# A new order of the ticks on every engine, in a transformer between two ternary FFNs

## The chip, the cores and the metric

One core of a Trainium2 chip. The time is that of the device in microseconds; before the change the median of three runs is 927.53 us (926.24 to 928.54).

## The reference, cut to what matters

The input is 16 sequences of 256 tokens, 128 features, in fp32: 4096 tokens, which the kernel cuts into 8 tiles of 512 tokens (two sequences each). Three parts follow one another, each with a residual:

```
x = x + 0.5 * ffn(layernorm(x))             # "input FFN"
x = x + layers(layernorm(x))                # 8 layers
x = x + 0.5 * ffn(layernorm(x))             # "output FFN"

def ffn(x):     # w_q is ternary: -1, 0, 1 by a threshold of mean |w|
    h = gelu(x / (rms(x) + eps) @ w_up_q.T)          # 128 -> 512, erf form
    return h / (rms(h) + eps) @ w_down_q.T           # 512 -> 128

for each of the 8 layers:
    Q = elu(x @ Wq + bq) + 1;  K = elu(x @ Wk + bk) + 1;  value = x @ Wv + bv
    KV = sum over the sequence of K * value;  Ksum = sum of K
    V = Q * KV / (Q * Ksum + eps)
    x = layernorm(gelu(V @ Wo + bo) + x) * scale + bias      # tanh form
    x = layernorm(gelu(gelu(x @ W1 + b1) @ W2 + b2) + x) * scale + bias
```

The sums run over one sequence only, so tile t of a layer needs tile t of the layer before and nothing else.

## The kernel before, in words

Layer work is 64 jobs (8 layers of 8 tiles), taken two at a time in 32 ticks. Each engine has a function that emits one tick (`tensor_tick`, `scalar_tick`, `vector_tick`, `gpsimd_tick`), and its last part is a list of calls, written out by hand. The queue of an engine is this list, tick after tick; it is worked off in order, and semaphores are all that holds the engines together.

A call such as `z(l(0, 3), 1)` names a stage, a tile and for some stages a half of the layer (0 attention, 1 FFN) or a chunk. `tiles_of` turns `l(k, lag)` into job 2 * (tick - lag) + k of the layers, `a(k, lag)` into a tile of the input FFN, t = 2 * (tick - lag + 4) + k, and `b(k, lag)` into one of the output FFN, t = 2 * (tick - lag - 32) + k. Where the number is out of range the call emits nothing. So a lag says how many ticks after the first a stage comes. `rest` leaves out tile 0 of the input FFN, whose first stages stand ahead of the ticks.

The stages of a layer tile, in the order of data: TensorE projects K, Q and V (`project`, three passes each); ScalarE makes the negative part and its `exp`; VectorE makes `round_kq`, `phi_k`, `phi_q`, `sum_kv` and the small `neg_ksum`, `over_ksum`, `sum_value`, `mean_v`; ScalarE `log_den` and `recip` (the reciprocal by ln and exp); VectorE `attend`; TensorE `project_o`; ScalarE `gelu_o`; VectorE `residual` 0; TensorE transposes (`turn_y`); VectorE `stats` and `means`; GpSimd `var_eps` and `rstd`; VectorE `z` (normalises, reading PSUM); TensorE turns back (`turn_z`); `full` applies scale and bias (ScalarE for half 0, VectorE for half 1); VectorE `hi` rounds and GpSimd `low` (L1303) takes the rest, for products in two parts; TensorE `up` (four chunks), ScalarE `gelu_h`, TensorE `down`, ScalarE `gelu_ff`, and from `residual` 1 on as above. GpSimd also splits the weights of the next layer, one piece (a cast, L1260, and a subtraction, L1262) behind `low(l(0, 3), 1)` and one behind it for the other tile.

An outer FFN tile: (`enter`, `x_in` at the output FFN: turns the layers' result and adds it to the token rows) `outer_stats`, `outer_means`, `var_eps`, GpSimd `sd` and `sd_eps`, VectorE `alpha`, ScalarE `normal`, TensorE `turn`, ScalarE `z_hi` (L678), VectorE `z_lo` (L953), TensorE `outer_up` (L531, L532), ScalarE `gelu` and `square`, VectorE `add_squares` (which sums the four chunks of squares into one, L1093 and L1095), TensorE `squares`, VectorE `mean_square`, GpSimd `rms`, VectorE `beta`, TensorE `outer_down` in two halves (L544), VectorE `outer_residual` (L1120). The input FFN goes on with `stats_c`, `means_c`, `rstd_c`, `z_c`, `turn_c`, `enter_full`, `enter_hi` and GpSimd's `x_low` (L1349), which together are the layer norm ahead of the layers.

The 8 banks of PSUM are shared: the dictionary `left` holds, for each bank, which semaphore says that it was drained, and `emptied` waits for it. SyncE only loads weights and inputs and stores the output; the change does not touch it. Where ScalarE goes over between `exp`/`ln` and a gelu, or between the two gelus, a table is loaded.

The lags before: input FFN -30 to -20, layers -1 to 3, output FFN 17 to 22, ticks from -34 to 57. Layer calls are in ticks -1 to 34, calls of the output FFN in ticks 49 to 57.

Of the kernel before, what the change touches and what calls it, by code (L numbers as in the profile page):

```python
# [680 lines left out]
def scalar_tick(act, m, s, f, tick, tables):  # L681
# [120 lines left out]
    gelu(b(1, 22), 0)
    gelu_h(l(1, 2), 1)
    z_hi(act, m, rest(a(1, -29)))
    gelu_ff(l(0, 2))
    gelu_o(l(1, 1))
    gelu_h(l(1, 2), 2)
    gelu(b(1, 22), 1)
    gelu_h(l(1, 2), 3)
    gelu(a(0, -29), 2)  # L810
    z_hi(act, m, b(0, 21))
    gelu(b(1, 22), 2)
    gelu(a(0, -29), 3)
    full(l(0, 1), 0)
    gelu(b(1, 22), 3)
# [13 lines left out]
    gelu(b(0, 21), 0)
    gelu(a(1, -29), 1)  # L830
    gelu(b(0, 21), 1)
    enter_full(a(0, -21))
    normal(act, m, rest(a(1, -30)))
    z_hi(act, m, b(1, 21))
    gelu_ff(l(1, 2))
    gelu(b(0, 21), 2)
    gelu(b(0, 21), 3)
    enter_hi(a(0, -21))
# [118 lines left out]
def vector_tick(dve, m, s, f, tick):  # L957
# [194 lines left out]
    add_squares(a(1, -27))  # L1152
    stats(l(1, 2), 0)
    means(l(0, 3), 1)
    round_kq(l(0, 0))
    over_ksum(l(1, 1))
    mean_square(b(0, 21))
    z_lo(dve, m, b(0, 20))
    x_in(b(1, 18))
    means(l(1, 2), 0)  # L1160
    phi_q(l(0, 0))
    outer_stats(dve, m, rest(a(0, -30)))
    beta(b(0, 21))
    alpha(dve, m, rest(a(0, -29)))
    beta(a(0, -27))
    outer_residual(a(0, -27))
# [242 lines left out]
```

## Time and profile before

| | us |
|---|---|
| median of three runs | 927.53 |
| lowest, highest | 926.24, 928.54 |
| the profiled execution | 928.71 |
| its span, first to last instruction | 926.9 |
| VectorE busy in the span | 823.6 (89%) |
| TensorE busy, matmuls | 855.2 (92%) |
| ScalarE busy | 795.8 (86%) |
| GpSimd busy | 443.4 (48%) |
| mean granted TensorE clock | 0.959 |

The busy shares are means over very unlike stretches: the opening and the input FFN (to about 108 us), the filling of the layers, the steady ticks, their drain (to about 839 us) and the output FFN. A granted clock of 1.00 is 2.4 GHz, 0.50 is 1.2 GHz. Names in rows are those of the buffers: `mv` is written by `means`, `st` by `stats`, `y` by `residual`, `kv` by `sum_value`, `nks` by `neg_ksum`, `fz_c` by `z_c`, `x_lo` by `low` or `x_low`, `x_tm` by `x_in` (L1085) or `outer_residual` (L1120).

### The profile page before, as it was taken

The numbers are of one execution on the slowest core, as the hardware profiler recorded it, in microseconds if no ns is written. First come the engines' busy times: TensorE is split into PE (matmuls) and PEld (weight loads), VectorE is DVE, ScalarE is ACT, GpSimd is POOL, SyncE is SP. The second block draws the span as 40 slices with busy tenths as digits, with TensorE's granted clock in tenths as the row PEclk, the third lists the DMA queues.
The fourth block names the chain that finished last, engine by engine and source line by source line (L and its number), as shares of the span: only waits on it lengthen the run. The fifth ranks groups of instructions, "written<-read, shape, count | busy, mean of one in ns | idle before, by whom it ended". The sixth has DMA issues, their size and how long they took to land.

```text
span 926.9 us, 14284 instructions
## 1 busy us (share of the span) xinstructions
PE 855.2 (92%) x3915; PEld 601.6 (65%) x3915; DVE 823.6 (89%) x3349; ACT 795.8 (86%) x1138; POOL 443.4 (48%) x561
## 2 busy tenths in 40 slices
PE   3898469999999999999999999999999999985897
PEld 2788245666666666666666666666666666654786
DVE  6677567999999999999999999999999999966663
ACT  3784579999999999999999999999999999733871
POOL 3253512555555555555555555555555555333230
PEclk8799789999999999999999999999999999995998
DMA  5000000000000000000000000000000000000011
GB/s 153 1 8 3 27 0 10 1 15 1 21 1 16 13 10 0 15 13 10 3 14 21 1 15 0 21 1 16 12 0 1 1 1 1 1 0 1 24 35 35
DMA packets 19518, 12.04 MB, mean 13 GB/s; under 512 B 1160, under 2 KB 18288, under 8 KB 19440
## 3 DMA queue, kind: packets, MB, share of 16 engines
q1 hardware_dynamic: 19440, 11.13, 4.2%
q8 instruction: 33, 0.54, 0.2%
q14 instruction: 45, 0.37, 0.1%
HBM read 9.03 MB, written 2.10 MB: 12 GB/s over the span
## 4 chain that ended last, share of the span: by engine, by line
DVE 69%; PE 12%; ACT 9%; issue 8%; POOL 2%; DMA 0%; DVEq 0%; ACTq 0%; POOLq 0%
DVE z L859 16%; DVE st L845 10%; DVE x_fm L1069 5%; DVE phi_k L982 5%; DVE kvf L993 4%; DVE phi_q L972 4%; DVE mv L852 4%; DVE e L965 4%; DVE vf L1034 3%; DVE x_hi L1077 3%; PE bank L544 3%; PE bank L394 2%; DVE y L1042 2%; ACT hsq L771 2%; ACT fh L764 2%
## 5 line engine op out<-in xcount | busy, mean ns | idle before, releaser
L1303 POOL TENSOR_TENSOR x_lo<-x_fm,x_hi 128x512 fp32r<-128x512 f32 x120 | 155.5, 1306 | 259.3 <-DVE x_hi L1077 259.3
L495 PE MATMUL bank<-h,w 128*128 128x512 f32 x512 | 260.5, 593 | 0.0
L737 ACT ACTIVATE h<-bank,par 128x512 f32<-128x512 f32 x256 | 167.1, 693 | 11.6 <-PE bank L402 10.6
L859 DVE TENSOR_SCALAR z<-bank,mv,rstd 128x128 f32<-128x128 f32 x512 | 169.2, 401 | 8.4 <-POOL rstd L1295 8.2
L400 PE MATMUL bank<-x_hi,w_hi 128*128 128x512 f32 x256 | 151.6, 592 | 1.6 <-ACT h L737 1.6
L1295 POOL TENSOR_TENSOR rstd<-ve,minus_half 128x4 f32<-128x4 f32 x128 | 132.8, 1037 | 10.7
L400 PE MATMUL bank<-x_hi,wqkv_hi 128*128 128x512 f32 x192 | 107.5, 560 | 11.2 <-DVE phi_q L972 10.1
L845 DVE BATCH_NORM_STATS2 st<-bank 128x6 f32<-128x128 f32 x512 | 112.8, 281 | 1.0 <-PE bank L394 0.9
L394 PEld LDWEIGHTS bank<-ident,y 128*128 128x128 f32 x512 | 62.3, 141 | 59.9 <-ACT x_fm L753 23.4
L402 PE MATMUL bank<-x_hi,w_lo 128*128 128x512 f32 x256 | 101.2, 395 | 0.0
L401 PE MATMUL bank<-x_lo,w_hi 128*128 128x512 f32 x256 | 101.1, 395 | 0.0
L495 PEld LDWEIGHTS bank<-h,w 128*128 128x128 f32 x512 | 86.9, 190 | 14.3 <-issue 3.4
L692 ACT ACTIVATE e<-bank,par 128x512 f32<-128x512 f32 x128 | 85.6, 693 | 8.0 <-PE bank L402 7.8
L1042 DVE TENSOR_TENSOR y<-bank,x_fm 128x512 f32<-128x512 f32 x128 | 86.9, 682 | 5.0 <-ACT bank L729 4.6
L1289 POOL TENSOR_SCALAR ve<-mv 128x4 f32<-128x4 f32 x128 | 49.5, 387 | 83.3 <-DVE mv L852 77.8
L656 ACT ACT_TABLE_LOAD x63 | 80.8, 1283 | 1.1
L394 PE MATMUL bank<-ident,y 128*128 128x128 f32 x512 | 77.4, 274 | 3.3 <-DVE y L1042 2.2
L737 ACT ACT_TABLE_LOAD x61 | 78.3, 1283 | 1.1
L402 PE MATMUL bank<-x_hi,wqkv_lo 128*128 128x512 f32 x192 | 78.0, 406 | 0.0
L401 PE MATMUL bank<-x_lo,wqkv_hi 128*128 128x512 f32 x192 | 78.0, 406 | 0.0
L400 PEld LDWEIGHTS bank<-x_hi,w_hi 128*128 128x128 f32 x256 | 48.6, 190 | 42.4 <-issue 17.2
L394 PE MATMUL bank<-ident,z 128*128 128x128 f32 x512 | 67.8, 275 | 7.4 <-DVE z L859 7.4
(102 smaller groups left out, 1780.7 us busy)
## 6 DMA issues: line engine op xcount, KB each, us to landing
x_tm<-in_x SPq DMA_DIRECT2D x8, 256.0 KB, 4.0
raw_w<-in_W SPq DMA_DIRECT2D x8, 256.0 KB, 2.7
w<-in_W SPq DMA_DIRECT2D x8, 256.0 KB, 2.9
out<-x_tm SPq DMA_DIRECT2D x8, 256.0 KB, 2.3
raw_qkv<-in_Wk SPq DMA_DIRECT2D x8, 64.0 KB, 2.0
raw_qkv<-in_Wq SPq DMA_DIRECT2D x8, 64.0 KB, 2.4
raw_qkv<-in_Wv SPq DMA_DIRECT2D x8, 64.0 KB, 2.3
wo<-in_Wo SPq DMA_DIRECT2D x8, 64.0 KB, 2.5
```

The source lines that it names most:

```text
L394: last = pe.transpose(bank[:, j * P:(j + 1) * P], src(j), m.ident[:, :])
L400: pe.matmul(bank[:, :], w_hi, x_hi, start=True, stop=False)
L401: pe.matmul(bank[:, :], w_hi, x_lo, start=False, stop=False)
L402: return pe.matmul(bank[:, :], w_lo, x_hi, start=False, stop=True)
L495: mm = pe.matmul(m.ps_o[:, :], m.w2[T.weights][:, c, :], m.h[:, T.par, c, :], start=c == 0, stop=c == FC - 1)
L692: act.activation(m.e[:, T.par, i, :], bank[:, :], ACT.Relu, bias=column(m, base, T.layer), scale=-1.0).then_inc(done, 1)
L737: act.activation(m.h[:, T.par, c, :], m.ps_h[c % 2][:, :], ACT.Gelu_apprx_tanh, bias=column(m, B1, T.layer, c, FC)).then_inc(s.gelu_h[T.pa ...
L845: last = dve.bn_stats(st[:, j, :], src(j))
L859: last = dve.tensor_scalar(dst[:, j, :], src(j), mv[:, j, 0:1], scale[:, j:j + 1], ALU.subtract, ALU.mult)
L1042: dve.tensor_tensor(m.y[i][:, T.par, :], (m.ps_v, m.ps_o)[i][:, :], m.x_fm[:, T.slot, :], ALU.add).then_inc((s.y1, s.y2)[i], 1)
L1295: pool.tensor_tensor(m.rstd[i][:, T.par, :], m.ve[i][:, T.par, :], m.minus_half[:, :], ALU.pow).then_inc((s.rstd1, s.rstd2)[i], 1)
L1303: pool.tensor_tensor(m.x_lo[:, T.slot, :], m.x_fm[:, T.slot, :], m.x_hi[:, T.slot, :].bitcast(F32), ALU.subtract).then_inc(done, 1)
```

## The change

It replaces the four lists, and the constants that say where the ticks begin and end. The stage functions, the buffers, the work of SyncE and what lies ahead of the ticks stay as they are, and each list has the same calls as before for the layers and both FFNs, in another order and with other lags. The lags now: input FFN -24 to -15, layers -2 to 3 (-2 only for one ScalarE call), output FFN -1 to 4; ticks from -28 to 39. So the calls of the output FFN stand in ticks 31 to 39, and the layers' in -2 to 34: in ticks 31 to 34 the lists of all engines hold both. The first layer's weight splits on GpSimd move from tick -29 to -23.

The constants, the new list of VectorE whole, before it that of TensorE whole, between them some lines of ScalarE's, and at the end that of GpSimd:

```diff
-TICK_QKV, TICK_W1 = -29, -29
-FIRST_TICK, END_TICK = -34, 58
+TICK_QKV, TICK_W1 = -23, -23
+FIRST_TICK, END_TICK = -28, 40
...
+    turn(pe, m, b(1, 3), left)
+    turn_z(l(0, 1), 0)
+    up(l(1, 2), 3)
+    turn_z(l(1, 3), 1)
+    outer_up(b(0, 3), 1)
+    outer_up(a(0, -21), 0)
+    outer_down(a(0, -20), 1)
+    outer_up(a(0, -21), 1)
+    project(l(1, 0), VALUE)
+    turn(pe, m, rest(a(1, -21)), left)
+    turn_c(a(1, -17))
+    squares(b(1, 4))
+    outer_up(b(0, 3), 2)
+    turn_y(l(0, 2), 1)
+    project(l(0, -1), KEY)
+    outer_up(b(0, 3), 3)
+    turn_y(l(1, 1), 0)
+    outer_up(a(0, -21), 2)
+    enter(b(0, -1))
+    project(l(0, -1), QUERY)
+    outer_down(b(1, 4), 0)
+    down(l(1, 2), 0)
+    outer_up(a(0, -21), 3)
+    outer_up(b(1, 3), 0)
+    squares(a(1, -20))
+    up(l(0, 1), 0)
+    outer_down(a(1, -20), 0)
+    outer_down(b(1, 4), 1)
+    outer_up(a(1, -21), 0)
+    outer_down(a(1, -20), 1)
+    down(l(1, 2), 1)
+    down(l(1, 2), 2)
+    outer_up(b(1, 3), 1)
+    turn(pe, m, b(0, 2), left)
+    project(l(0, -1), VALUE)
+    down(l(1, 2), 3)
+    outer_up(a(1, -21), 1)
+    outer_up(b(1, 3), 2)
+    outer_up(b(1, 3), 3)
+    project(l(1, -1), KEY)
+    enter(b(1, -1))
+    squares(b(0, 3))
+    project(l(1, -1), QUERY)
+    up(l(0, 1), 1)
+    up(l(0, 1), 2)
+    turn_z(l(1, 1), 0)
+    turn_z(l(0, 2), 1)
+    project_o(l(0, 0))
+    up(l(0, 1), 3)
+    outer_down(b(0, 3), 0)
+    turn(pe, m, rest(a(0, -22)), left)
+    turn_y(l(1, 2), 1)
+    down(l(0, 1), 0)
+    outer_up(a(1, -21), 2)
+    outer_up(b(0, 2), 0)
+    outer_up(a(1, -21), 3)
+    turn_y(l(0, 0), 0)
+    turn_c(a(0, -18))
+    outer_down(b(0, 3), 1)
+    down(l(0, 1), 1)
+    project_o(l(1, 0))
+    up(l(1, 1), 0)
+    down(l(0, 1), 2)
+    up(l(1, 1), 1)
+    down(l(0, 1), 3)
+    up(l(1, 1), 2)
+    squares(a(0, -21))
+    outer_down(a(0, -21), 0)
...
+    gelu(b(0, 3), 3)
+    square(b(0, 3))
+    exp(l(1, -1))
...
+    normal(act, m, b(0, 2))
+    gelu(b(1, 3), 0)
...
+    z_hi(act, m, b(0, 2))
...
+    square(a(0, -21))
+    gelu(b(1, 3), 2)
+    normal(act, m, rest(a(0, -22)))
+    gelu(b(1, 3), 3)
+    gelu(a(1, -21), 0)
...
+    normal(act, m, rest(a(1, -22)))
+    normal(act, m, b(1, 2))
...
+    z(l(0, 3), 1)
+    outer_stats(dve, m, rest(a(1, -23)))
+    mean_v(l(1, 1))
+    var_eps(dve, m, b(1, 2))
+    sum_kv(l(0, 0))
+    mean_square(a(1, -20))
+    attend(l(1, 1))
+    residual(l(1, 3), 1)
+    alpha(dve, m, b(0, 2))
+    z_lo(dve, m, rest(a(1, -21)))
+    means_c(a(1, -19))
+    stats_c(a(0, -20))
+    alpha(dve, m, rest(a(0, -22)))
+    hi(l(1, 2), 0)
+    full(l(0, 3), 1)
+    residual(l(0, 1), 0)
+    stats(l(1, 3), 1)
+    beta(a(1, -20))
+    hi(l(0, 3), 1)
+    means(l(1, 3), 1)
+    sum_value(l(0, 0))
+    over_ksum(l(0, 0))
+    stats(l(0, 1), 0)
+    add_squares(a(0, -21))
+    means(l(0, 1), 0)
+    z_lo(dve, m, b(1, 3))
+    var_eps_c(a(0, -19))
+    outer_stats(dve, m, b(1, 1))
+    z(l(1, 3), 1)
+    mean_v(l(0, 0))
+    x_in(b(1, 0))
+    beta(b(1, 4))
+    z(l(0, 1), 0)
+    round_kq(l(1, 0))
+    residual(l(1, 1), 0)
+    add_squares(b(0, 3))
+    alpha(dve, m, rest(a(1, -22)))
+    var_eps_c(a(1, -19))
+    phi_k(l(1, 0))
+    outer_residual(b(1, 4))
+    outer_means(dve, m, rest(a(0, -23)))
+    outer_means(dve, m, b(0, 1))
+    residual(l(0, 2), 1)
+    outer_residual(a(1, -20))
+    neg_ksum(l(1, 0))
+    var_eps(dve, m, rest(a(0, -23)))
+    full(l(1, 3), 1)
+    hi(l(0, 1), 0)
+    alpha(dve, m, b(1, 2))
+    outer_means(dve, m, rest(a(1, -23)))
+    z_lo(dve, m, rest(a(0, -22)))
+    z_c(a(0, -19))
+    mean_square(a(0, -21))
+    var_eps(dve, m, rest(a(1, -23)))
+    phi_q(l(1, 0))
+    sum_kv(l(1, 0))
+    mean_square(b(0, 3))
+    over_ksum(l(1, 0))
+    hi(l(1, 3), 1)
+    z_lo(dve, m, b(0, 2))
+    add_squares(b(1, 3))
+    stats(l(0, 2), 1)
+    outer_stats(dve, m, rest(a(0, -24)))
+    stats_c(a(1, -20))
+    stats(l(1, 1), 0)
+    beta(a(0, -21))
+    sum_value(l(1, 0))
+    add_squares(a(1, -21))
+    attend(l(0, 0))
+    means(l(1, 1), 0)
+    beta(b(0, 3))
+    round_kq(l(0, -1))
+    means(l(0, 2), 1)
+    x_in(b(0, -1))
+    outer_residual(b(0, 3))
+    var_eps(dve, m, b(0, 1))
+    phi_k(l(0, -1))
+    outer_stats(dve, m, b(0, 0))
+    outer_means(dve, m, b(1, 1))
+    outer_residual(a(0, -21))
+    z_c(a(1, -19))
+    means_c(a(0, -20))
+    phi_q(l(0, -1))
+    mean_square(b(1, 3))
+    z(l(1, 1), 0)
+    neg_ksum(l(0, -1))
...
+    sd(b(1, 2))
+    var_eps(l(0, 1), 0)
+    sd_eps(b(1, 2))
+    sd_eps(a(1, -23))
+    rstd(l(0, 1), 0)
+    low(l(0, 3), 1)
+    rms(a(1, -21))
+    split_next_qkv(l(0, 0))
+    split_next_w1(l(0, 0))
+    rms(b(0, 3))
+    split_next_qkv(l(1, 0))
+    split_next_w1(l(1, 0))
+    low(l(0, 1), 0)
+    rstd_c(a(0, -20))
+    sd(b(0, 1))
+    low(l(1, 3), 1)
+    rstd_c(a(1, -20))
+    var_eps(l(1, 1), 0)
+    rstd(l(1, 1), 0)
+    sd(a(0, -24))
+    var_eps(l(0, 2), 1)
+    rstd(l(0, 2), 1)
+    sd_eps(b(0, 1))
+    x_low(a(1, -15))
+    rms(a(0, -22))
+    low(l(1, 1), 0)
+    var_eps(l(1, 2), 1)
+    sd_eps(a(0, -24))
+    sd(a(1, -24))
+    rms(b(1, 3))
+    rstd(l(1, 2), 1)
+    x_low(a(0, -16))
```

## Rows read from the trace of the kernel before

**Rows 1.** The page, 40 slices of the span, busy tenths of VectorE.
```profile
DVE  6677567999999999999999999999999999966663
```
**Rows 2.** Stretches: bounds and length in us, then busy us (x instructions) of PE, PEld, DVE, ACT, POOL.
```profile
0.00:160.00 160.00, 113.86 (x590) 89.88 (x591) 107.41 (x429) 106.00 (x158) 58.77 (x80) 0.86 0.10 29
160.00:782.00 622.00, 622.00 (x2676) 419.90 (x2674) 620.31 (x2562) 608.44 (x856) 340.14 (x430) 1.00 0.03 8
782.00:839.00 57.00, 49.84 (x208) 31.66 (x207) 45.54 (x177) 31.53 (x45) 20.72 (x27) 0.95 0.00 1
839.00:853.00 14.00, 7.22 (x29) 5.25 (x29) 10.46 (x50) 4.42 (x10) 5.92 (x6) 0.50 0.00 1
853.00:927.00 74.00, 62.30 (x418) 54.86 (x416) 39.89 (x135) 45.40 (x72) 17.84 (x18) 0.92 0.09 29
```
**Rows 3.** Instructions in time order, VectorE: start us, us, line and operation [idle before].
```profile
261.98 0.72 DVE L972 SCALAR_TENSOR_TENSOR phi_q<-bank,par,e 128x512 f32<-128x512 f32 x1
```
**Rows 4.** The same view, one steady tick of VectorE.
```profile
459.26 2.63 DVE L859 TENSOR_SCALAR z<-bank,mv,rstd 128x128 f32<-128x128 f32 x8
461.82 0.47 DVE L982 SCALAR_TENSOR_TENSOR phi_k<-bank,par,e 128x256 f32<-128x256 f32 x1
...
474.17 0.21 DVE L1015 SCALAR_TENSOR_TENSOR kv<-ksum,par,kvacc 128x2 f32<-128x2 f32 x1
...
474.36 0.68 DVE L1042 TENSOR_TENSOR y<-bank,x_fm 128x512 f32<-128x512 f32 x1
...
479.27 0.88 DVE L845 BATCH_NORM_STATS2 st<-bank 128x6 f32<-128x128 f32 x4
480.18 0.38 DVE L852 BATCH_NORM_AGGREGATE mv<-st 128x2 f32<-128x6 f32 x4
480.48 0.72 DVE L972 SCALAR_TENSOR_TENSOR phi_q<-bank,par,e 128x512 f32<-128x512 f32 x1
```
**Rows 5.** The same view, VectorE in the drain, the last layer tile.
```profile
833.64 0.38 DVE L852 BATCH_NORM_AGGREGATE mv<-st 128x2 f32<-128x6 f32 x4
835.49 1.36 DVE L859 TENSOR_SCALAR z<-bank,mv,rstd 128x128 f32<-128x128 f32 x4 [1.47 <-POOL rstd L1295]
```
**Rows 6.** The same view, VectorE and GpSimd at the end of the input FFN.
```profile
95.21 1.12 DVE L859 TENSOR_SCALAR fz_c<-x_tm,fmv_c,frstd_c 128x128 f32<-128x128 f32 x4
96.53 4.88 DVE L859 TENSOR_SCALAR fz_c<-x_tm,fmv_c,frstd_c 128x128 f32<-128x128 f32 x4 [0.20 <-POOL frstd_c L1341]
...
96.39 9.87 POOL L1349 TENSOR_TENSOR x_lo<-x_fm,x_hi 128x512 fp32r<-128x512 f32 x8
```
**Rows 7.** The same view, GpSimd in a steady tick: the cast of a weight split.
```profile
461.35 0.29 POOL L1260 CAST w_hi<-raw_w 128x128 fp32r<-128x128 f32 x1
```
**Rows 8.** The same view, TensorE and VectorE between layers and output FFN.
```profile
837.00 1.08 PE L394 MATMUL bank<-ident,z 128*128 128x128 f32 x4 [4.45 <-DVE z L859]
837.88 1.06 PE L394 MATMUL bank<-ident,x_fm 128*128 128x128 f32 x4
...
852.95 0.78 PE L531 MATMUL bank<-zc_hi,upT 128*128 128x512 f32 x1
...
838.13 0.81 DVE L1069 TENSOR_SCALAR x_fm<-bank,par 128x512 f32<-128x512 f32 x1 [1.27 <-PE bank L394]
```
**Rows 9.** The same view, the output FFN at its pace, and the last residual.
```profile
883.72 0.50 PE L531 MATMUL bank<-zc_hi,upT 128*128 128x512 f32 x1 [0.99 <-DVE zc_lo L953]
...
898.83 0.51 PE L531 MATMUL bank<-zc_hi,upT 128*128 128x512 f32 x1 [0.98 <-DVE zc_lo L953]
...
922.79 1.12 DVE L1120 SCALAR_TENSOR_TENSOR x_tm<-bank,scale,x_tm 128x128 f32<-128x128 f32 x4 [5.26 <-PE bank L544]
```
**Rows 10.** Groups from 782 us on: line, engine, operation xcount | busy us, mean ns | idle before.
```profile
L678 ACT ACTIVATE zc_hi<-bank 128x512 fp32r<-128x512 f32 x8 | 4.8, 601 | 1.5 <-PE bank L394 1.5
...
L1085 DVE TENSOR_TENSOR x_tm<-bank,x_tm 128x512 f32<-128x512 f32 x8 | 5.5, 686 | 1.7 <-PE bank L394 1.6
L953 DVE TENSOR_TENSOR zc_lo<-bank,zc_hi 128x512 fp32r<-128x512 f32 x8 | 5.5, 686 | 2.8 <-ACT zc_hi L678 2.8
```

More of the change, by code:

```diff
@@ L802, in scalar_tick @@
[L802 to L815, printed above, removed]
     negative(l(0, -1), QUERY)
-    negative(l(0, -1), KEY)
+    recip(l(0, 0))
     exp(l(0, -1))
-    square(b(1, 22))
-    square(a(0, -29))
-    normal(act, m, b(1, 21))
@@ L822, in scalar_tick @@
-    normal(act, m, rest(a(0, -30)))
+    z_hi(act, m, rest(a(0, -21)))
+    gelu(b(0, 3), 0)
     log_den(l(1, 0))
-    recip(l(0, 0))
+    gelu(b(0, 3), 1)
     recip(l(1, 0))
-    gelu(a(1, -29), 0)
     gelu_h(l(0, 1), 0)
-    gelu_h(l(0, 1), 1)
[L829 to L838, printed above, removed]
@@ L839, in scalar_tick @@
-    negative(l(1, -1), QUERY)
-    enter_full(a(1, -21))
+    gelu_ff(l(1, 2))
+    z_hi(act, m, b(1, 3))
+    negative(l(1, -1), KEY)
+    gelu(a(1, -20), 2)
+    gelu(a(1, -20), 3)
+    gelu_h(l(0, 1), 1)
+    square(a(1, -20))
+    gelu_h(l(0, 1), 2)
+    gelu(b(0, 3), 2)
+    full(l(1, 1), 0)
+    gelu(a(0, -21), 0)
+    gelu(a(0, -21), 1)
+    gelu_o(l(0, 0))
+    enter_hi(a(1, -16))
+    negative(l(1, -1), QUERY)
+    gelu_h(l(0, 1), 3)
+    gelu(b(0, 3), 3)
+    square(b(0, 3))
+    exp(l(1, -1))
@@ new lines, in scalar_tick @@
+    z_hi(act, m, rest(a(1, -21)))
+    gelu_o(l(1, 0))
+    gelu_h(l(1, 1), 0)
+    gelu(a(0, -21), 2)
+    gelu_h(l(1, 1), 1)
+    normal(act, m, b(0, 2))
+    gelu(b(1, 3), 0)
+    gelu(a(0, -21), 3)
+    enter_full(a(0, -17))
+    gelu(b(1, 3), 1)
+    z_hi(act, m, b(0, 2))
+    enter_hi(a(0, -17))
+    gelu_ff(l(0, 1))
+    gelu_h(l(1, 1), 2)
+    full(l(0, 0), 0)
+    square(a(0, -21))
[3 more added lines that the diff above has]
+    gelu(a(1, -21), 0)
@@ L843, in block_stats @@
+    gelu_h(l(1, 1), 3)
+    gelu(a(1, -21), 1)
+    log_den(l(0, -1))
+    square(b(1, 3))
+    normal(act, m, rest(a(1, -22)))
+    normal(act, m, b(1, 2))
+    enter_full(a(1, -17))
+    negative(l(0, -2), KEY)
 def block_stats(dve, src, st, done):
@@ L1150, in z_c @@
         normalise(dve, m.fz_c[:, F.par], token_source(m, F), m.fmv_c[:, F.par], m.frstd_c[:, F.par], F.f.z_c)
[L1152 to L1166, printed above, removed]
@@ L1194, in vector_tick @@
     hi(l(1, 2), 0)
     full(l(0, 3), 1)
-    mean_square(b(1, 21))
+    residual(l(0, 1), 0)
     stats(l(1, 3), 1)
+    beta(a(1, -20))
     hi(l(0, 3), 1)
-    outer_means(dve, m, rest(a(0, -30)))
     means(l(1, 3), 1)
-    round_kq(l(1, 0))
-    x_in(b(0, 17))
-    var_eps(dve, m, rest(a(0, -30)))
-    stats(l(0, 1), 0)
-    means_c(a(0, -27))
-    means(l(0, 1), 0)
-    phi_q(l(1, 0))
-    outer_stats(dve, m, rest(a(1, -30)))
-    z(l(1, 3), 1)
-    z_lo(dve, m, b(1, 20))
-    z(l(0, 1), 0)
@@ L1212, in vector_tick @@
-    outer_stats(dve, m, b(1, 18))
-    phi_k(l(1, 0))
-    residual(l(0, 2), 1)
-    outer_residual(a(1, -27))
-    sum_value(l(0, 0))
-    residual(l(1, 1), 0)
-    neg_ksum(l(1, 0))
-    full(l(1, 3), 1)
-    mean_v(l(0, 0))
-    beta(b(1, 21))
-    hi(l(0, 1), 0)
-    mean_square(a(0, -28))
-    outer_means(dve, m, rest(a(1, -30)))
-    var_eps_c(a(0, -27))
-    stats_c(a(1, -27))
+    sum_value(l(0, 0))
[3 more added lines that the diff above has]
+    means(l(0, 1), 0)
@@ L1230, in vector_tick @@
-    z_lo(dve, m, rest(a(0, -29)))
-    outer_residual(b(1, 21))
-    add_squares(b(0, 20))
-    sum_kv(l(1, 0))
-    alpha(dve, m, b(1, 19))
-    var_eps(dve, m, b(0, 18))
-    var_eps(dve, m, rest(a(1, -30)))
-    add_squares(b(1, 20))
+    outer_stats(dve, m, rest(a(0, -24)))
[9 more added lines that the diff above has]
+    means(l(0, 2), 1)
```

123 lines of the change are left out of this document (removed).

## The prediction

> **What bounds the kernel now.** I read first the page's busy shares and 40 slices, then a table of stretches, then single instructions in time order. The slices of VectorE stand at 9 from about 140 us to 790 us and at 5 to 8 outside [rows 1]. The stretches say how full that is: from 160 to 782 us VectorE is busy 620.31 of 622 us and TensorE 622.00 of 622, ScalarE 608.44 [rows 2]. There the order can lose time and hardly win any. Outside, VectorE idles 160 - 107.4 = 53 us before 160 us, 57 - 45.5 = 11 us while the last layer drains, 3.5 us in the 14 us behind it and 74 - 39.9 = 34 us in the rest of the output FFN [rows 2]. All gains must come from these 101 us. One tick of two tiles is ten ticks apart at 261.98 and 480.48 us, so 21.85 us [rows 3, 4]; some 29 of them are in the steady stretch (622/21.85).
>
> **What the change keeps.** The steady lists have the same calls: 32 on TensorE, 24 on ScalarE, 40 on VectorE, and the same four activation-table loads a tick (two `exp` groups between gelus). Nothing is added or taken away, DMAs included; an empty entry of a tick issues nothing, so shorter lags (first tick -28, last 39) cost or save nothing by themselves. Everything is position within the queues.
>
> **Steady ticks, rstd waits: +6 us.** A normalisation `z` needs `rstd` of GpSimd, which needs `means`. A `means` started at 833.64 us and the `z` behind it at 835.49, with VectorE waiting 1.47 us for `rstd`: 1.85 us from start to start [rows 5]. In the old order `phi_q` or more stands between the two. In the new one, after `means(l(1,3),1)` come `sum_value`, `over_ksum`, `stats(l(0,1),0)`, `means(l(0,1),0)`, then `z(l(1,3),1)`. By start-to-start times of the trace: 0.30 (480.18 to 480.48) + 0.19 (474.17 to 474.36, `sum_value` and one such small instruction) + 0.91 (479.27 to 480.18) + 0.30 = 1.70 us [rows 4]. That is 0.15 us short of 1.85. Then `z(l(0,1),0)` stands 0.30 + 0.15 + 1.28 + 0.07 (the small `mean_v`, less than half of that 0.19) = 1.80 us behind the start of its own `means`, the 1.28 being half of 2.56 us for two `z` (459.26 to 461.82) [rows 4]: 0.05 us short. Together 0.20 us on a queue that has no slack: 29 x 0.20 = 6 us. Bounds: 0 (if a pair of instructions runs a little longer than my rows and covers it) and 0.3 a tick, 9 us. Other chains I compared in the same manner (`hi` after `full`, `turn_z` after `z`, the residual before the next `down`) have as much room as they had, and TensorE has the 0.20 us as slack then.
>
> **Steady ticks, GpSimd against VectorE: +1.5 us.** In the opening, `z_c` of one tile took 1.12 us, that of the next 4.88 us while GpSimd ran eight `x_low` back to back (9.87 us, 1.23 each): every quarter waited for one of them [rows 6]. So a VectorE instruction that reads and writes SBUF alone can be held up for the rest of a GpSimd instruction. Of this kind are `round_kq`, `hi` and `attend`. In the new tick, `low(l(0,3),1)` starts together with `z(l(0,1),0)`, both released by the same `rstd`; its follower on GpSimd, 1.23 us later, is the 0.29 us cast of a weight split [rows 6, 7], and `round_kq(l(1,0))` comes 1.28 us later [rows 4], 0.05 us into that cast. Cost between 0 and 0.3 us a tick. `hi(l(1,3),1)` follows `hi(l(0,1),0)` by `phi_q` and `sum_kv`, about as long as the `x_low` that the first one releases, so it may touch its end: 0 to 0.1 more. I take 0.05 a tick, since the two come so close that a shift of 0.3 us undoes it: 1.5 us; bounds 0 and 0.4 a tick, 12 us.
>
> The Trainium skill (SBUF — State Buffer, section "SBUF: two separate sides") says that the port pair shared by VectorE and GpSimd is an exclusive lock held for the whole instruction, the first to start winning and the other blocking. The trace agrees (4.88 against 1.12 us). It speaks against this change: taken to the letter, each tick would pay the rest of the cast at least, and that is the first rival below.
>
> **Drain, 782 to 839 us: +2.5 us.** `enter`, `x_in` and `outer_stats` of the output FFN now stand inside ticks 31 to 34, from lag -1 on. VectorE has 11 us of idle time there [rows 2]; TensorE 7. Before its last `down` TensorE gets five more `enter`: groups of four transposes start 0.88 us apart at half clock (837.00 to 837.88 [rows 8]), so 0.44 at full clock, 2.2 us, and a little where `x_in` stands before a `z`. Bounds 0 (hidden) and +6 (eight `x_in` of 0.69 us [rows 10] all on the chain, and some statistics).
>
> **The hand-over to the output FFN: -10 us.** Now the last `full` starts at 838.13 us, and the first `outer_up` at 852.95: 14.8 us in which six more `x_in`, statistics, roots, `alpha`, `normal`, `turn`, `z_hi` and `z_lo` of tile 0 pass one after another, TensorE at a granted 0.50, that is 1.2 GHz [rows 8, 2]. In the new lists tile 0 has had statistics and roots by tick 33, and `alpha`, `normal` run beside the last layer tile's chain of tick 34. What stays behind the last `turn_z` is, at half clock: `enter` of tile 6 (0.88), `turn` (1.08), `z_hi` 0.60, `z_lo` 0.69, `x_in` 0.69, `enter` of tile 7 (0.88) [rows 8, 10], 4.8 us, against 852.95 - 838.08 (end of the last `turn_z`) = 14.9. So -10. Bounds -6 and -13.
>
> **Pace of the outer FFNs: -4 us.** Two tiles take 898.83 - 883.72 = 15.1 us at the end, of which TensorE waits 0.98 us for `z_lo` [rows 9]. The new order puts `outer_down` of the other tile between `turn` and the `outer_up` that needs `z_lo`, which covers it: 14.1 to 14.4 us a pair, over three pairs of the output FFN and about as many of the input FFN, -2 us each. Bounds 0 and -8. The end is as before: `squares` and `outer_down` of the last tile behind `outer_residual` of the last but one, with the 5.26 us wait before the last residual [rows 9]. The first tile's gelu still stands behind `normal` of tile 1, and the eight `turn_c` still run after the last square: opening otherwise 0, with ±4 for it and for the filling of the layer pipeline, where even tiles now run half a tick earlier.
>
> **Sum.** 6 + 1.5 + 2.5 - 10 - 4 = -4 us. The profiled execution took 928.71 us (span 926.9, 1.8 around it), 1.2 above the median of 927.53: 924.7 for it, 923.5 for the median. I give 924.
>
> **Rivals.** (1) Slower: the exclusion of the two engines decides. If `round_kq(l(1,0))` waits 0.3 us in each tick and `hi` 0.1, with the 0.2 of `rstd` a tick is 22.45 us, +17 us; with +2.5 - 10 - 4 that is +6, 933 us. The change turns slower from 0.4 us a tick on (11.5/29). For it: the cast stands right at that place in every tick with a split; against: it is 0.29 us short, and the two starts need only drift 0.3 us apart. (2) The steady tick stays at 21.85, because small durations shift, and the rest comes: -11.5 to -16, 913 us. For it: GpSimd is half idle (340 of 622 us [rows 2]); against: 1.85 is measured on an idle GpSimd and can't be shorter. (3) The change doesn't overlap what it means to: the in-order queues couple drain and output FFN (`x_in` of tile 4 before `z(l(0,3),1)`), the drain grows by 6 to 8 us and eats the hand-over: 927 to 930.
>
> **Chances.** Forecast 0.45 (alone 919 to 929), rival 1 0.22, rival 2 0.20, rival 3 0.13. The range 910 to 934 leaves out the far ends of rivals 1 and 2. A measurement of this kernel tells 0.3%, 2.8 us, from no change: faster than 924.75 gets 0.26 of the forecast's 0.45, all of rival 2 and 0.03 of rival 3, 0.49; slower than 930.3 gets 0.02, 0.18 and 0.03, 0.23; the rest, 0.28, is within.
>
> **What would show it.** In the profile after: `phi_q` of one tile ten ticks apart by 220.5 us (22.05 a tick), with VectorE waits for `rstd` in the steady stretch, about two a tick and 0.15 and 0.05 us; `round_kq` rows that are longer than before are rival 1's. Some 4 to 6 us between the start of the last `full` and the first `outer_up` of the output FFN, where 14.8 stood. Pairs there 14.1 to 14.4 us apart. The forecast is wrong if the steady tick is under 21.9 or over 22.3 us, if the hand-over stays above 9 us, or if opening and filling move by more than 5 us.

## The result, and the profile after

The changed kernel takes 919.31 us (median of 7 runs, 918.08 to 923.22) against 927.14 for the kernel before (7 runs, 926.24 to 928.89): ratio 0.9918, 95% interval 0.9900 to 0.9936. The profiled execution took 919.31 us with a span of 917.5.

The slices of the page, to be read against [rows 1], and the stretches:

```profile
DVE  6688557999999999999999999999999999988674
PEclk9899569999999999999999999999999999999899
```

```profile
0.00:160.00 160.00, 117.12 (x601) 91.44 (x602) 110.05 (x443) 107.62 (x161) 60.19 (x81) 0.86 0.10 29
160.00:770.00 610.00, 609.75 (x2585) 405.83 (x2584) 606.56 (x2479) 592.15 (x826) 328.91 (x421) 1.00 0.03 8
```

VectorE is nearly as full as before (606.56 of 610 us, 99.4%; before 620.31 of 622, 99.7% [rows 2]), yet two tiles now take longer. One tile's `phi_q` starts at 199.97 and, 24 ticks later, at 732.19 us: 22.18 us a tick, where it was 21.85 [rows 3, 4]. The loss shows in VectorE's and GpSimd's rows of one tick, in order of time; idle time under a few tenths gets no bracket, so the reader subtracts starts:

```profile
479.91 0.37 DVE L852 BATCH_NORM_AGGREGATE mv<-st 128x2 f32<-128x6 f32 x4
480.19 0.18 DVE L1015 SCALAR_TENSOR_TENSOR kv<-ksum,par,kvacc 128x2 f32<-128x2 f32 x1
480.30 0.16 DVE L1008 RECIPROCAL nrk<-nks 128x2 f32<-128x2 f32 x1
480.38 0.87 DVE L845 BATCH_NORM_STATS2 st<-bank 128x6 f32<-128x128 f32 x4
481.28 0.38 DVE L852 BATCH_NORM_AGGREGATE mv<-st 128x2 f32<-128x6 f32 x4
481.75 1.37 DVE L859 TENSOR_SCALAR z<-bank,mv,rstd 128x128 f32<-128x128 f32 x4
483.03 0.15 DVE L1024 TENSOR_TENSOR neg_a<-kv,nrk 128x2 f32<-128x2 f32 x1
483.18 1.37 DVE L859 TENSOR_SCALAR z<-bank,mv,rstd 128x128 f32<-128x128 f32 x4
484.46 0.71 DVE L965 TENSOR_SCALAR e<-e 128x1024 f32<-128x1024 f32 x1
485.10 0.68 DVE L1042 TENSOR_TENSOR y<-bank,x_fm 128x512 f32<-128x512 f32 x1
```

```profile
480.67 1.04 POOL L1295 TENSOR_TENSOR rstd<-ve,minus_half 128x4 f32<-128x4 f32 x1
481.80 0.23 POOL L1289 TENSOR_SCALAR ve<-mv 128x4 f32<-128x4 f32 x1
482.11 1.04 POOL L1295 TENSOR_TENSOR rstd<-ve,minus_half 128x4 f32<-128x4 f32 x1
483.12 1.28 POOL L1303 TENSOR_TENSOR x_lo<-x_fm,x_hi 128x512 fp32r<-128x512 f32 x1
484.33 0.29 POOL L1260 CAST wqkv_hi<-raw_qkv 128x128 fp32r<-128x128 f32 x1
```

`means` at 481.28 is followed 0.47 us later, 0.30 in the order before [rows 4]: `z` waits 0.17 for the `rstd` that ends at 481.71. The small `mean_v` at 483.03 is followed after 0.15, not 0.07: the second `z` waits 0.08 for the `rstd` that ends at 483.15. The `round_kq` beside the cast is followed after 0.64 instead of 0.58. Averaged over 22 ticks of each profile, from start to start, it is +0.20 us a tick behind `means`, +0.08 behind `mean_v`, +0.06 behind `round_kq`, +0.05 behind the two `phi_q`, and -0.07 over all the rest: 0.32. These rows say where the time stands, not yet what taking one of them away would bring.

Behind the layers the time comes back. The last `full`, the first `outer_up` of the output FFN, and the last two residuals, against [rows 8, 9]:

```profile
847.22 0.81 DVE L1069 TENSOR_SCALAR x_fm<-bank,par 128x512 f32<-128x512 f32 x1 [0.39 <-PE bank L394]
```

```profile
851.98 0.78 PE L531 MATMUL bank<-zc_hi,upT 128*128 128x512 f32 x1
```

```profile
908.28 1.13 DVE L1120 SCALAR_TENSOR_TENSOR x_tm<-bank,scale,x_tm 128x128 f32<-128x128 f32 x4
...
913.41 1.13 DVE L1120 SCALAR_TENSOR_TENSOR x_tm<-bank,scale,x_tm 128x128 f32<-128x128 f32 x4 [2.43 <-PE bank L544]
```

The balance of the two profiles, in us, from such starts (before, after): up to the first `round_kq` 108.39, 104.05, that is -4.3; from there to the `phi_q` of job 11, counted from 0, some five ticks on (the "tenth" of two expectations below), 109.9, 118.1, +8.2 (6.6 of it beside five times 0.32); from that to the last job's `phi_q` (26 ticks) 568.0, 576.3, +8.3; drain to the last `full` 51.9, 48.8, -3.1; to the first `outer_up` 14.8, 4.8, -10.1; from it to the first residual 17.8, 15.4, -2.4; six more residuals 44.1, 40.9, -3.2; to the last one 8.0, 5.1, -2.8. Sum -9.4, as the spans.

The granted clock goes with the loss of the filling. The 24 us from the first `round_kq` on, first in the kernel before, then in the changed one (the last number but two is the clock):

```profile
108.00:132.00 24.00, 12.18 (x32) 7.09 (x32) 14.15 (x55) 16.53 (x23) 0.38 (x2) 0.86 0.09 25
104.00:128.00 24.00, 15.40 (x32) 9.37 (x32) 13.19 (x55) 13.96 (x20) 0.00 (x0) 0.51 0.08 24
```

### The profile page after: what moved, and what is told of

Read it like the earlier page. It is cut to its first block, busy times and chain, and to the rows that moved or that the text cites. A ratio compares the mean times of both kernels' runs of the same rounds, so it can differ in the third digit from the quotient of the medians.

```text
span 917.5 us, 14284 instructions
## 1 busy us (share of the span) xinstructions
PE 857.4 (93%) x3915; PEld 596.7 (65%) x3915; DVE 830.0 (90%) x3349; ACT 800.4 (87%) x1138; POOL 441.2 (48%) x561
## 4 chain that ended last, share of the span: by engine, by line
DVE 67%; PE 16%; issue 6%; ACT 5%; POOL 5%; DMA 0%; SPq 0%; DVEq 0%; ACTq 0%; POOLq 0%
DVE z L859 15%; DVE st L845 8%; DVE y L1042 8%; PE bank L544 6%; DVE phi_k L982 5%; DVE phi_q L972 4%; DVE e L965 4%; DVE x_fm L1069 4%; POOL rstd L1295 4%; DVE kvf L993 4%; DVE x_hi L1077 3%; DVE vf L1034 3%; DVE mv L852 3%; PE bank L394 2%; PE bank L531 2%
## 5 line engine op out<-in xcount | busy, mean ns | idle before, releaser
L1303 POOL TENSOR_TENSOR x_lo<-x_fm,x_hi 128x512 fp32r<-128x512 f32 x120 | 153.6, 1280 | 225.5 <-DVE x_hi L1077 225.5
L495 PE MATMUL bank<-h,w 128*128 128x512 f32 x512 | 255.5, 592 | 0.0
L859 DVE TENSOR_SCALAR z<-bank,mv,rstd 128x128 f32<-128x128 f32 x512 | 174.0, 403 | 7.9 <-POOL rstd L1295 5.2
L737 ACT ACTIVATE h<-bank,par 128x512 f32<-128x512 f32 x256 | 169.5, 690 | 9.1 <-PE bank L402 7.9
L400 PE MATMUL bank<-x_hi,w_hi 128*128 128x512 f32 x256 | 160.9, 629 | 0.0
L1295 POOL TENSOR_TENSOR rstd<-ve,minus_half 128x4 f32<-128x4 f32 x128 | 132.7, 1037 | 10.7
L400 PE MATMUL bank<-x_hi,wqkv_hi 128*128 128x512 f32 x192 | 108.6, 565 | 12.7 <-DVE phi_k L982 11.9
L495 PEld LDWEIGHTS bank<-h,w 128*128 128x128 f32 x512 | 91.7, 189 | 31.3 <-issue 17.5
L845 DVE BATCH_NORM_STATS2 st<-bank 128x6 f32<-128x128 f32 x512 | 109.8, 281 | 2.2 <-PE bank L394 2.2
L1289 POOL TENSOR_SCALAR ve<-mv 128x4 f32<-128x4 f32 x128 | 39.9, 312 | 129.2 <-DVE mv L852 124.1
L394 PE MATMUL bank<-ident,z 128*128 128x128 f32 x512 | 73.9, 277 | 9.0 <-DVE z L859 9.0
L394 PEld LDWEIGHTS bank<-ident,z 128*128 128x128 f32 x512 | 59.5, 141 | 29.4 <-DVE z L859 11.2
```

Source lines behind the costliest of these rows:

```text
L394: last = pe.transpose(bank[:, j * P:(j + 1) * P], src(j), m.ident[:, :])
L400: pe.matmul(bank[:, :], w_hi, x_hi, start=True, stop=False)
L495: mm = pe.matmul(m.ps_o[:, :], m.w2[T.weights][:, c, :], m.h[:, T.par, c, :], start=c == 0, stop=c == FC - 1)
L737: act.activation(m.h[:, T.par, c, :], m.ps_h[c % 2][:, :], ACT.Gelu_apprx_tanh, bias=column(m, B1, T.layer, c, FC)).then_inc(s.gelu_h[T.pa ...
L845: last = dve.bn_stats(st[:, j, :], src(j))
L859: last = dve.tensor_scalar(dst[:, j, :], src(j), mv[:, j, 0:1], scale[:, j:j + 1], ALU.subtract, ALU.mult)
```

## The experiments

**The three parts by themselves.** The lists of each engine were spliced: input FFN, layers and output FFN from either kernel.

```diff
 # e3: input and output FFN of the kernel before; layers' calls in the new order
 # e6: the kernel before; only the input FFN's calls a(...) in the new order,
 #     with their new lags and first tick
 # e4: the changed kernel, output FFN behind the layers
-    outer_up(b(0, 3), 1)
+    outer_up(b(0, 21), 1)      # all b(...) of all engines by +18 ticks
```

> The kernel before with only the calls of the layers in the new order; the input FFN ahead of them and the output FFN behind them keep their old order, and nothing of the output FFN stands inside the layers. Theory: this part alone is a loss: 31 ticks of +0.32 us = +10, a filling that takes +5, a drain of -3: 927 + 12 = 937 to 941 us; tick 22.17. Rival 1 (the loss of the filling is only the price of the earlier start of the layers, that is of something late that both kernels wait for): the filling costs 0 to 1 here and the time is 933 to 936. Rival 2 (the longer tick comes of the empty or changed surroundings, or of another placement in the run): tick 21.85 and 926 to 928.

Measured: 940.41 us, ratio 1.0143 (1.0123 to 1.0163), so +13 us, as expected. Tick 22.17, first `round_kq` at 108.28 as before, job 11's `phi_q` 8.2 us later than before, drain 48.0. The loss of the filling is not a price of an earlier start: rival 1 falls. The new order of the layers is a loss wherever it stands.

> The kernel before with the calls of the input FFN alone in their new order; the layers and the output FFN keep the old one. Theory (three parts that add up): the opening gains 4 to 6 us up to the first round_kq (108.4 us before, 101.7 to 104.1 in the four profiles with the new order), and because the layers' filling and steady stretch are those of before, all of it reaches the end: 922 to 924 us. Rival (the filling takes it back: what comes later is bound by something else than the input FFN): 926 to 928 us, with the first phi_q early and the tenth where it was, at 218.3 us.

Measured: 924.16 us (919.94 to 925.21), ratio 0.9961 (0.9946 to 0.9976): -2.4 us between the medians, -3.6 by the ratio. The profiled run is one of the quickest, 920.12. In its profile the first `round_kq` is at 102.13, and the last `full` at 832.83, 5.3 us earlier than before: in this run what the input FFN gained reached the last `full`. Over all runs it is 2 to 4 us.

> The changed kernel with the lags of all calls of the output FFN raised by 18 ticks, so that it stands wholly behind the layers, in its new order. Theory (the overlap gives the hand-over, the order gives the pace and the end): from the last full to the first outer_residual 30 to 33 us instead of 20.1, that is +10 to +12; the drain 0 to 2 us shorter; then pairs of 13.7 us and a last residual 5.1 us behind the one before as in the changed kernel: 929 to 931 us. Rival (pace and end are gained because the overlap keeps TensorE's granted clock up): pairs of 15 us and 8 us at the end as well, 935 to 938 us.

Measured: 932.00 us, 1.0056 (1.0039 to 1.0073), 12.7 above the changed kernel. From the last `full` at 844.29 to the last residual at 926.05 it takes 81.8 us, not 66.2. All 15.6 us lie ahead of the first residual: the seven gaps behind it are those of the changed kernel (7.3 and 6.4, the last 5.1). So the overlap makes the hand-over, and the order makes the pace. From the last `full` to the first residual it takes 35.7 us, where 30 to 33 stood: the granted clock is 0.50 all the way from 840 to 860 us here, and eight `enter` pass one by one, seven of them waiting for an `x_in`. How much of the 15.6 is the low clock and how much the overlap is not told apart here; a pair of runs with the clock up, below, does that.

**Where the tick loses.** One call of VectorE's list is moved into the wait for `rstd`.

```diff
     means(l(0, 1), 0)
+    round_kq(l(1, 0))
     ...
     z(l(0, 1), 0)
-    round_kq(l(1, 0))
```

> The changed kernel with one VectorE call moved: round_kq(l(1, 0)) goes from behind z(l(0, 1), 0) to ahead of z(l(1, 3), 1), right behind means(l(0, 1), 0). Theory (waits for rstd): the two normalisations come 1.84 and 1.90 us behind the start of their means in the changed kernel, with about 0.17 and 0.08 us of waiting in each tick, and 0.06 more for the rounding that runs beside the cast of a weight split. With 0.6 us of work put between, both waits and that overlap go: tick 22.17 to about 21.9, 30 ticks, -7 to -9 us, so 911 us, and VectorE shows z directly behind round_kq. Rival A (the tick is longer for other reasons, such as phi_q of 741 instead of 717 ns or TensorE's order): the tick stays at 22.1 to 22.2 and the time at 918 to 920. Rival B (z comes 0.6 us later and TensorE, which is full as well, has to wait for it): the tick grows beyond 22.2, 920 to 925.

Measured: 947.95 us, 1.0231 (1.0209 to 1.0253). All three theories missed; rival B has the longer tick, but neither its size nor its cause. The tick is 23.13 us (453.66 to 476.79 of one `phi_q`). VectorE and GpSimd in that run, columns as above:

```profile
469.31 0.69 DVE L965 TENSOR_SCALAR e<-e 128x1024 f32<-128x1024 f32 x1
469.92 1.36 DVE L859 TENSOR_SCALAR z<-bank,mv,rstd 128x128 f32<-128x128 f32 x4
471.20 1.27 DVE L1024 TENSOR_TENSOR neg_a<-kv,nrk 128x2 f32<-128x2 f32 x1
472.39 0.72 DVE L859 TENSOR_SCALAR z<-bank,mv,rstd 128x128 f32<-128x128 f32 x2
```

```profile
469.47 0.61 POOL L1289 TENSOR_SCALAR ve<-mv 128x4 f32<-128x4 f32 x1
470.17 1.04 POOL L1295 TENSOR_TENSOR rstd<-ve,minus_half 128x4 f32<-128x4 f32 x1
471.18 1.27 POOL L1303 TENSOR_TENSOR x_lo<-x_fm,x_hi 128x512 fp32r<-128x512 f32 x1
```

Both waits for `rstd` are gone (`z` at once behind `round_kq`). But `mean_v`, two columns wide, now comes 0.02 us behind the start of an `x_low` and takes 1.27 instead of 0.15 us; in the changed kernel it comes 0.09 ahead of it. All 28 long rows of `mean_v` in this run (1.26 to 1.28 us) begin 0.01 or 0.02 us behind an `x_low` and end within 0.02 us of it. The loss is 1.12 us for 0.11 us in position, and the tick is 0.96 longer than in the changed kernel. It goes the other way too: `ve` beside `round_kq` takes 0.61, not 0.23. The Trainium skill (SBUF — State Buffer, section "SBUF: two separate sides") names a VectorE operation with two SBUF inputs, which `mean_v` is, against a GpSimd operation that reads SBUF: the second one blocks for the whole instruction. The trace agrees, 1.27 beside 1.27. For `round_kq` beside the cast it does not come out in full: in the changed kernel 0.17 us of the cast are left in each tick when `round_kq` starts, and its row is 0.06 longer (0.72, against 0.66 for the other one).

```diff
     means(l(0, 1), 0)
+    mean_v(l(0, 0))
+    round_kq(l(1, 0))
     ...
     z(l(1, 3), 1)
-    mean_v(l(0, 0))
     ...
-    round_kq(l(1, 0))
```

> The changed kernel with two VectorE calls moved: mean_v(l(0, 0)) and round_kq(l(1, 0)) both stand between means(l(0, 1), 0) and z(l(1, 3), 1). In the run with round_kq alone in that place the tick was 23.13 us, and the small mean_v (128x2), which came 1.28 us behind the start of z, took 1.27 us instead of 0.15, in the time of one x_low of GpSimd (1.28 us) that the same rstd had released. Theory (exclusion of VectorE and GpSimd, whole instructions long): with mean_v ahead of rstd nothing of SBUF alone stands in the reach of x_low; the tick is 23.13 - 1.12 = 22.01 us, 0.16 below the changed kernel's 22.17, and the time 919.3 - 31 x 0.16 = 914 us (911 to 916). Rival (mean_v was long for another reason, a semaphore for example): it is 1.27 us in its new place too, tick 23.1 and 948 us. Rival (it was no wait for rstd that made the changed kernel's tick long): tick 22.17, 919 us.

Measured: 918.69 us, 0.9919 (0.9905 to 0.9934): no change against the changed kernel. `mean_v` is short again, 0.12 to 0.16 us in all its rows, so that it was the neighbour on GpSimd and not a semaphore; but the tick is 22.12 us, where 22.01 was expected. With both waits for `rstd` gone, only 0.05 of their 0.25 us came back. A piece of VectorE and ScalarE:

```profile
490.08 0.37 DVE L852 BATCH_NORM_AGGREGATE mv<-st 128x2 f32<-128x6 f32 x4
490.49 0.70 DVE L965 TENSOR_SCALAR e<-e 128x1024 f32<-128x1024 f32 x1
```

```profile
489.42 1.04 ACT L700 ACTIVATE e<-e 128x1024 f32<-128x1024 f32 x1
```

The other `round_kq` now waits for ScalarE's `exp`, which ends at 490.46: 0.41 behind `means` instead of 0.29. The next releaser was only some 0.1 us less late than `rstd`.

```diff
-    round_kq(l(0, -1))
     means(l(0, 2), 1)
+    round_kq(l(0, -1))
```

> The run with mean_v and round_kq ahead of z, and one more VectorE call moved: round_kq(l(0, -1)) goes behind means(l(0, 2), 1). In the run before this one the tick was 22.12 us and not 22.01, and this round_kq began at 490.49 us, 0.41 behind the start of the means ahead of it instead of 0.29, just as ScalarE's exp (489.42, 1.04 us) ended; GpSimd's ve ran 0.73 instead of 0.23 us beside it. Theory (with the rstd waits gone, ScalarE's exp is the next that is late, by 0.12 us): with the means between, exp has 0.29 us more, the tick falls to 22.00 us, -4 us, 914 to 916. Rival (ScalarE is full and its loop is the bound, so that VectorE's order doesn't matter any more): tick 22.10 to 22.15, 918 to 919. Rival (the ve of the second means is held up by round_kq and rstd comes late): tick over 22.2, 922.

Measured: 919.80 us, 0.9918 (0.9904 to 0.9932), tick 22.10. The wait for `exp` is gone (492.00 behind an `exp` that ended at 491.82), but `phi_k`, now directly behind the `round_kq` it needs, starts 0.69 us behind it instead of 0.58. The rival with the full loop holds as to the tick; which loop sets 22.10, ScalarE's, TensorE's or another one, was not settled.

```diff
     low(l(0, 3), 1)
-    split_next_qkv(l(0, 0))    # and the three other split calls
     ...
     rstd(l(0, 2), 1)
+    split_next_qkv(l(0, 0))    # and the three others
```

> The changed kernel with the four calls of the weight splits moved on GpSimd, from behind low(l(0, 3), 1) to behind rstd(l(0, 2), 1), a stretch in which GpSimd idles for 4 us and VectorE works on PSUM. Theory (the exclusion of the two engines is a small term): round_kq(l(1, 0)) gets back to 0.58 to 0.60 us from start to start, the mean of L965 from 687 to about 660 ns, the tick 22.17 to 22.11, -2 us, 917.5. Rival (the exclusion decides): the tick falls to 21.9 and the time to 911. Rival (GpSimd's later splits hold up var_eps of the next tick and with it rstd): slower than the changed kernel, 920 to 925.

Measured: 922.64 us, 0.9953 (0.9935 to 0.9971). The tick fell to 22.14 and the mean `round_kq` from 687 to 670 ns, about half of what the theory gave (22.11 and 660). The end was 3 us worse all the same. In the profile the last `full` is 1.3 us earlier than in the changed kernel and the first `outer_up` 4.8 us behind it as there, but from the last `full` to the first residual it takes 24.7 us instead of 20.1. The stretches behind it, first of this run, then of the changed kernel (the last number but two is the granted clock):

```profile
855.00:859.00 4.00, 1.88 (x6) 0.59 (x4) 2.75 (x7) 3.68 (x6) 0.00 (x0) 0.93 0.00 0
859.00:863.00 4.00, 3.29 (x12) 2.94 (x13) 1.65 (x9) 3.18 (x7) 0.00 (x0) 0.50 0.00 0
863.00:867.00 4.00, 4.00 (x20) 4.00 (x21) 2.50 (x4) 3.59 (x6) 2.72 (x2) 0.50 0.00 0
```

```profile
856.00:860.00 4.00, 1.57 (x6) 0.67 (x4) 3.08 (x7) 3.97 (x7) 0.00 (x0) 1.00 0.00 0
860.00:864.00 4.00, 3.37 (x25) 3.06 (x26) 2.35 (x11) 3.91 (x8) 0.63 (x1) 1.00 0.00 0
864.00:868.00 4.00, 4.00 (x35) 3.84 (x34) 2.83 (x7) 3.08 (x6) 1.35 (x2) 1.00 0.00 0
```

The same work meets 1.2 GHz in one run and 2.4 GHz in the other. Why the clock fell here is not shown; no weight split runs in this stretch. The time lies in the last rival's range, but the tick got shorter, so it is not by that rival's way.

**The clock.** Idle transposes, whose result nobody reads, were put where TensorE waits.

```diff
+def spin(pe, m, left, n):
+    emptied(pe, left, "h1")
+    for j in range(n):
+        pe.transpose(m.ps_h1[:, 0:P], m.ident[:, :], m.ident[:, :])
 # e7: spin 28 ahead of the last turn_z, 12 ahead of enter of tile 7, 16 ahead of turn of tile 2
 # e8: spin 8 ahead of each turn_c (last 14); 20, 12, 14 ahead of the first projection of jobs 1 to 3
```

> The changed kernel with idle transposes of the identity on TensorE, whose result nobody reads: 28 ahead of the last layer tile's wait for z (4.6 us of idle time), 12 ahead of the enter of tile 7, 16 ahead of the turn of tile 2 in the output FFN. Theory (the granted clock decides part of the hand-over): in the changed kernel the granted clock is 0.50 from 846 to 855 us, in the run with the later splits also from 859 to 869, where the first outer_residual came 24.7 us behind the last full instead of 20.1. With TensorE busy the clock stays at 1.00, the enters and turns take 0.63 instead of 1.1 us and the first outer_up 0.4 instead of 0.6: -2 to -4 us for the median, 915 to 917, and the spread between runs of one kernel (918.1 to 923.2) shrinks. Rival (the added work stands in the way, or the clock falls all the same): 919 to 921 us.

Measured: 917.56 us (915.11 to 917.77), 0.9898 (0.9881 to 0.9915). The granted clock is 1.00 from 840 to 870 us, for example:

```profile
848.00:852.00 4.00, 3.12 (x21) 2.30 (x19) 3.02 (x15) 3.97 (x8) 2.38 (x3) 1.00 0.00 0
```

From the last `full` to the first residual 18.0 us, 2.1 less than in the changed kernel. All five runs lie below the lowest of the changed kernel (918.08), by 0.3 to 3.0 us; the intervals of the two ratios overlap. The median is 0.6 above the theory's range.

> The changed kernel with idle transposes of the identity on TensorE while the pipeline of the layers fills: 8 ahead of each turn_c (14 ahead of the last), and 20, 12 and 14 ahead of the first projection of jobs 1 to 3, where TensorE waits 4.0, 2.4 and 2.8 us. Theory (the filling is a chain at half clock: nine matmuls of a job take 3.9 us from 112.4 to 116.4 at a granted 0.50): at full clock they take 2.2, three jobs -4 to -5 us up to the first steady tick, of which half reaches the end: 915 to 917 us. Rival (the filling is set by ScalarE's and VectorE's chain of the first jobs, and TensorE's part is hidden): 918 to 921 us, the tenth phi_q where it was, at 222 us.

Measured: 918.96 us, 0.9912 (0.9893 to 0.9931). In the profile the granted clock from 104 to 128 us is 0.92, where it was 0.51; the stretch from the first `round_kq` to job 11's `phi_q` is 2.1 us shorter, and the last `phi_q` 2.75 us earlier. The hand-over, which has no transposes here, took 1.7 us more. The time is in the rival's range, and the gain isn't told from zero by itself.

```diff
 # e10: layers' calls of the kernel before, a(...) and b(...) of the changed one, b(...) by +18 ticks
 # e11: e10 with the transposes of e7 and e8, and 8 ahead of each enter but the first
 # e12: e9 with the transposes of e7 and e8
```

> A splice: the layers in the old order, input FFN and output FFN in the new one, but the output FFN wholly behind the layers. Theory (the parts add up): the kernel before, 927, -5 for the input FFN (the run with that alone was 5.3 us ahead at the last full), and for the output FFN what the run with the raised lags showed against the kernel before, 81.8 us from the last full to the last residual against 84.7: -3; 918 to 920 us, the same as the changed kernel: the new order of the layers loses what its overlap gains. Rival (the new order of the output FFN needs the new order of the layers to be quick): 923 to 926.

Measured: 924.07 us, 0.9957 (0.9936 to 0.9978), and the widest spread of all: 917.4 to 926.9, with mean granted clocks of 0.961 for the two quickest runs and 0.950 for the slowest. Tick 21.85, 83.3 us from the last `full` to the last residual. The median was expected 4 to 6 us lower; it lies in the rival's range (923 to 926), and only the two quickest runs (917.4 and 917.7) are where the sum puts it. The profiled run (925.96) is among the longer ones: 37.2 us from the last `full` to the first residual at a mean clock of 0.57, against 32.6 in the kernel before; behind that the pace is the changed kernel's, so the rival is not right about the pace. The output FFN's new order, put wholly behind the layers, begins later and runs faster.

> The same splice with the idle transposes on TensorE of the two warm runs: 8 ahead of each turn_c (14 ahead of the last), 20, 12 and 14 ahead of the first projection of jobs 1 to 3, 28 ahead of the last layer tile's wait for z, 8 ahead of each enter but the first, 16 ahead of the turn of tile 2. Theory (the clock decides part of the filling and of the hand-over): at a granted 1.00 seven enters cost 0.44 less each (1.1 against 0.63 us), the first outer_ups and turns 2 to 4 us less, the filling 2.6: 5 to 9 us below the splice alone, 910 to 914. Rival (VectorE's and ScalarE's chain sets the hand-over, and 8 transposes are longer than the wait): -2 us at most, 916 to 918.

Measured: 920.48 us, 0.9932 (0.9915 to 0.9949), a miss. From the last `full` to the first residual 28.7 instead of 37.2 us, at a granted 1.00, so the hand-over gained 8.5; but the last `phi_q` came 5.7 us later than in the splice, all of it before job 11's `phi_q`: with the old order of the layers the transposes in the filling cost time. A mean clock of 0.979 did not make this kernel quicker than the changed one at 0.970. The hand-over now has its clock at 1.00 both with the output FFN overlapped (18.0 us, the run with the warm end) and behind the layers (28.7 us here): some 10.7 us are the overlap's without the clock, though the order of the layers differs too.

> The changed kernel with what its runs gave put together: mean_v(l(0, 0)) and round_kq(l(1, 0)) ahead of z(l(1, 3), 1), round_kq(l(0, -1)) behind means(l(0, 2), 1), and the idle transposes of the filling and of the hand-over. Theory (three gains that add up): 31 ticks of 22.10 instead of 22.17 us are -2.2, the warm hand-over took the last full to the first outer_residual from 20.1 to 18.0 us, -2, the warm filling brought the last phi_q forward by 2.7 us: 919.3 - 7 = 912.5 us (911 to 915). Rival (the filling's gain is a matter of which stretches the clock falls in, and doesn't last over runs): 915 to 917 us.

Measured: 911.03 us (907.76 to 911.54), 0.9814 (0.9796 to 0.9832): 8 us below the changed kernel, within the theory's range, and the best of all. Last `phi_q` at 792.69 instead of 798.43, tick 22.09, 18.0 us from the last `full` to the first residual.

## Why the prediction was right, and where it was not

The waits for `rstd` and the hand-over came nearly as forecast, in size and by their path, and the total lies within the range: 919.31 us, with 924 forecast, 910 to 934 stated and 919 to 929 for the forecast alone. That the total is near is in part luck: the differences from the sum's terms, listed at the end, are +9.0 us on one side and -14.4 on the other. The tick of 22.17 rules out the second rival, which has 21.85, and a drain that got shorter the third.

**Steady ticks, waits for `rstd`.** Right in place and mechanism, 0.17 and 0.08 us where 0.15 and 0.05 stood. The five instructions from the first `means` to its `z` take 1.67 us without the wait, not 1.70, and the second `z` starts 1.90 us behind its `means`, not 1.85: the 0.05 a tick that the sum fell short. What it left out: taking the waits away isn't worth their length. Without them the tick is still 22.12, with `exp` the next that is late, and 22.10 without that one; so what most of the 0.32 us hangs on is open.

**GpSimd against VectorE.** 0.06 us a tick at the named place, predicted 0.05. The tick was forecast at 22.05 and is 22.17. The two terms, 0.20 and 0.05 on 21.85, make 22.10; the 22.05 leaves the second one out. The longer `phi_q` (741 ns, before 717) was not foreseen either. Rival 1 was nearer than the chance said: `mean_v`, which the prediction didn't look at, runs 0.09 us ahead of an `x_low`, and e1 shows what it costs if it doesn't.

**Drain.** Wrong in sign: -3.1, predicted +2.5. In e3 and e4, where nothing of the output FFN stands in the drain, it is 48.0 us; so the overlap costs 0.8 where 2.5 stood, and the new order of the layers drains 3.8 faster, which the sum put at nothing. By which of its calls is not shown.

**Hand-over.** 4.8 us from the last `full` to the first `outer_up`, -10.1, and by the path that was worked out: `enter`, `turn`, `z_hi`, `z_lo`, `x_in`, `enter`, at a granted 0.50. **Pace.** Pairs of 13.65 us where 14.1 to 14.4 were forecast; -3.2 and -2.4 ahead of it, for -2. **The end** was said to stay; it gave -2.8. TensorE's `outer_down` of the last tile ran at a granted 1.00; before, the mean between the last two residuals was 0.57. With the old order of the output FFN that gap is 7.95 us at 0.57, 6.48 at 0.74 (e3) and 5.13 at 1.00 (e6), so its length goes with the clock. The new order has 5.1 us in each of its eleven profiles; whether it is what keeps the clock up is not shown.

**Opening and filling.** -4.3, then +6.6 beyond the longer ticks; predicted -2 and 0, with ±4. The filling alone moved by more than the 5 us that the prediction named as a sign of being wrong, the two together by +2.3. The filling's term was put at nothing without rows. e3 shows that it comes with the new order of the layers; of the 6.6 us, 2 to 4 go with the clock (118.1 against 116.0 us in e8, 117.5 in e9 against 113.7 in e12, each time with the clock up; with the old order a clock of 0.66 in the first 24 us went with 1.0 more, 110.9 in e6 against 109.9), and the cause of the rest is open. Against the sum's terms the measured ones differ by +2.4 (steady), +6.6 (filling), -2.3 (opening), -5.6 (drain), -3.6 (pace behind the hand-over), -2.8 (end) and -0.1 (hand-over): -5.4 together, so -9.4 where -4 was forecast. A reading to put right: the slices of VectorE [rows 1] stand at 9 from 162 to 811 us, and at 3 to 7 outside.

## What to carry over

Price an order by starts, not by durations, and for every small operation on two SBUF tensors ask what GpSimd does in the microsecond around it: 0.11 us of position decided over 28 us, 947.95 against 919.31. When several loops of a full tick are within 0.1 us of each other, moving one wait gives back little; here nearly all that was gained came at the ends: the opening, the filling, the drain, the hand-over and the last tile. There, look at the granted clock before comparing two orders.
